# Group sums from TensorE to VectorE, one expert's product added by a DMA, and image 0's epilogue in halves

## The reference, cut to what matters

```python
def _gn(v, G=32, eps=1e-05):            # mean and variance over 4 channels and the plane
    g = v.reshape(B_, G, C_ // G, H_, W_)
    ...
# block 1, on n = gn(x): a convolution mixed from four experts by image
routing = sigmoid(mean(n, (2, 3)) @ w_route.T + b_route)          # (16, 4)
y = conv3x3(n, w_experts)                                         # 4 experts, 128 -> 128
out = einsum('beohw,be->bohw', y, routing)
h = x + silu(batchnorm(out))
# block 2, on n = gn(h): a convolution with the signs of W
result = h + conv3x3(gn(h), sign(W))
```

## Time and profile before

| what | value |
|---|---|
| median of three runs | 272.57 us |
| the profiled execution, its own time | 272.72 us |
| its span | 270.6 us |
| PE busy | 263.6 us, 97% |
| DVE busy | 254.6 us, 94% |
| ACT busy | 213.0 us, 79% |
| POOL busy | 45.5 us, 17% |
| granted TensorE clock | full in all 40 slices (2.4 GHz) |
| DMA queue of POOL (q0), share of the 16 DMA engines | 33.1% |

### The profile page before, as it was taken

The page is one execution under the profiler, slowest core; times in us unless marked ns, Lnnn a source line. Parts: engine busy times, 40 slices in busy tenths (PEclk is TensorE's granted clock), DMA queues, the critical chain, the costliest instruction groups (busy, mean ns, idle before and its releaser), DMA issues.

```text
span 270.6 us, 4214 instructions
## 1 busy us (share of the span) xinstructions
PE 263.6 (97%) x1339; PEld 182.5 (67%) x1339; DVE 254.6 (94%) x461; ACT 213.0 (79%) x469; POOL 45.5 (17%) x61
## 2 busy tenths in 40 slices
PE   8899999999999999999999999999999999999993
PEld 7554857668595766759486776849576675948573
DVE  5799999999999999999999999999999999995984
ACT  2798898898979787997979798897979796736860
POOL 2012120313121120312112021212112021210120
PEclk9999999999999999999999999999999999999999
DMA  6998945552617355452726456261735536272407
GB/s 202 417 388 279 325 150 156 78 155 32 127 78 131 104 79 155 58 134 54 145 80 97 136 79 159 27 128 80 125 108 80 157 47 128 70 136 87 78 2 155
DMA packets 10245, 35.20 MB, mean 130 GB/s; under 512 B 1264, under 2 KB 1904, under 8 KB 10224
## 3 DMA queue, kind: packets, MB, share of 16 engines
q0 software_dynamic: 4176, 15.21, 33.1%
q1 hardware_dynamic: 5616, 19.34, 19.1%
q10 hardware_dynamic: 432, 0.39, 0.4%
HBM read 11.34 MB, written 16.25 MB: 102 GB/s over the span
## 4 chain that ended last, share of the span: by engine, by line
PE 95%; DVE 2%; issue 1%; POOL 0%; ACT 0%; DVEq 0%; POOLq 0%
PE pc L599 43%; PE pa L562 14%; PE pb L562 14%; PE pe_ L562 14%; PE pd L552 6%; PE pd L488 2%; PE ps L531 1%; PE ps L535 1%; DVE U L1178 0%; PE pa L636 0%; PE pb L636 0%; DVE X L1404 0%; PE pc L521 0%; POOL rstd L446 0%; DVE sums L1386 0%
## 5 line engine op out<-in xcount | busy, mean ns | idle before, releaser
L1188 DVE SCALAR_TENSOR_TENSOR U<-we,route,U 128x1152 f32<-128x1152 f32 x45 | 63.7, 1415 | 0.5
L599 PE MATMUL pc<-lo,ws 128*128 128x496 f16 (+3 forms) x270 | 62.0, 375 | 0.0
L599 PE MATMUL pc<-hi,ws 128*128 128x496 f16 (+3 forms) x270 | 59.8, 375 | 0.1
L599 PEld LDWEIGHTS pc<-hi,ws 128*128 128x128 f16 x270 | 26.4, 98 | 29.6 <-issue 0.5
L599 PEld LDWEIGHTS pc<-lo,ws 128*128 128x128 f16 x270 | 27.7, 106 | 26.3
L446 POOL TENSOR_TENSOR rstd<-ve,nhalf 128x2 f32<-128x2 f32 (+1 forms) x19 | 17.5, 923 | 141.4 <-ACT ve L856 120.1
L562 PE MATMUL pa<-V,UM 128*128 128x256 f32 (+1 forms) x180 | 40.7, 375 | 0.0
L562 PE MATMUL pb<-V,UM 128*128 128x256 f32 (+1 forms) x180 | 40.6, 375 | 0.0
L562 PE MATMUL pe_<-V,U 128*128 128x256 f32 (+1 forms) x180 | 40.5, 375 | 0.0
L562 PEld LDWEIGHTS pb<-V,UM 128*128 128x128 f32 x180 | 34.1, 190 | 5.5 <-issue 0.7
L562 PEld LDWEIGHTS pe_<-V,U 128*128 128x128 f32 x180 | 34.2, 190 | 3.9
(11 more groups left out here) (168 smaller groups left out, 400.9 us busy)
## 6 DMA issues: line engine op xcount, KB each, us to landing
X<-x SPq DMA_DIRECT2D x15, 512.0 KB, 5.6
out<-X SPq DMA_DIRECT2D x15, 512.0 KB, 2.6
out<-ev POOLq DMA_DIRECT2D x15, 512.0 KB, 5.5
X<-y POOLq DMA_DIRECT2D x14, 512.0 KB, 4.5
we<-w_experts SPq DMA_DIRECT2D x2, 768.0 KB, 8.2
ws_raw<-w_sign SPq DMA_DIRECT2D x1, 576.0 KB, 10.4
we<-w_experts SPq DMA_DIRECT2D x1, 512.0 KB, 6.2
out<-X SPq DMA_DIRECT2D x1, 384.0 KB, 3.0
```

The source lines that it names most:

```text
L599: mm = mm_(rows[:, r0 - first // W:r1 - first // W, c0:c1], ws[:, tap * C:(tap + 1) * C], plane((hi, lo)[part], i)[:, r0 + ky - 1:r1 + ky ...
L1188: v.scalar_tensor_tensor(out=nine(U[i % RING]), in0=expert(e), scalar=route[:, i, e:e + 1], in1=nine(U[i % RING]), op0=ALU.mult, op1=ALU.a ...
```

## The change

Five things are changed.

1. **Group sums on DVE.** For the chains 4 to 17 `group_stats` on PE goes. DVE does `group_sums(c)` instead: a shuffle of the four columns with partition p^1, an add, a shuffle with p^2, an add, each waiting for the one before by a semaphore. It stands behind `inner_rows(t+1)` (in slot 15 ahead of `sign_points`). `variances`, `deviation` and `centring` read the sums from SBUF with a factor 1/4; `bias` reads a copy `gmid` that a new ACT instruction makes (`middle_mean`).
2. **Expert 1 by ACT and a DMA.** For the images 3 to 15 DVE's `mix(i, 1)` goes. ACT writes route[1]*expert 1 to a tile `scaled` (`scale_second`, last in its slot) and POOL issues a DMA that adds it to U (`add_scaled`, last in POOL's slot).
3. **hi sooner.** ACT does `bias` and `split_hi` ahead of `deviation`, `centring` and `pads`.
4. **Image 0 in halves.** SiLU and residual of image 0 are done in two halves of the plane; the residual stands ahead of `all_rows(2)` in DVE's order.
5. **Signs in two parts**, four taps ahead of `variance(2)` and five between the SiLU halves.

`route_logits` also waits for the previous chain's `th`.

```diff
+SCALED_FROM = 3
+        def first_mix(i):
+            return 2 if i >= SCALED_FROM else 1
+        def by_shuffles(c):
+            return LAG < c < CHAINS - 1
+        def group_means(c, a, b):
+            return (gsum[:, c, a:b], 1.0 / GSIZE) if by_shuffles(c) else (gstats(c, a, b), 1.0)
...
# POOL
+            def add_scaled(i):
+                pool.wait_ge(mix_first, firsts_before(i) + 1)
+                pool.wait_ge(scaled_ready, i - SCALED_FROM + 1)
+                g.dma_start(flat(U[i % RING][:]), scaled[:], accum_op=ALU.add).then_inc(scaled_added, 16)
...
                 if ND <= t < B and t not in DVE_RESIDUAL:
                     residual(t)
+                if t + LAG - 1 < B:
+                    add_scaled(t + LAG - 1)
...
# PE, slot t
                 if t < B:
                     minus_points(t)
                     if t > 1:
-                        group_stats(c)
                         sign_half(t - 2, 1, 1, TAP_ORDER[-1:])
...
# ACT
+            def wait_group(c):
+                if by_shuffles(c):
+                    act.wait_ge(gsum_ready, c - LAG)
+                else:
+                    act.wait_ge(gvar_ready, c + 1)
...
+            def middle_mean(c):
+                activation(gmid[:, c:c + 1], gsum[:, c, MID:MID + 1], ACT.Copy, scale=1.0 / GSIZE) \
+                    .then_inc(gmid_ready, 1)
...
+            def scale_second(i):
+                wait(act, scaled_added, 16 * (i - SCALED_FROM))
+                activation(scaled[:].rearrange("p (g n) -> p g n", n=C), expert(1), ACT.Copy,
+                           scale=route[:, i, 1:2]).then_inc(scaled_ready, 1)
...
+            def first_silu(half):
+                act.wait_ge(bn_ready, 5)
+                act.wait_ge(direct_ready, half + 1)
+                activation(flat3(y[0][:])[:, half * BANK:(half + 1) * BANK], direct_bank(0)[:, half, :], ACT.Silu,
+                           bias=bn_shift[:, 0:1], scale=bn_direct[:, 0:1],
+                           accum_out=(ysum[:, 0:1], first_ysum[:])[half]).then_inc(silu_ready, 1)
...
             centring(2)
+            sign_weights(0, 4)
             variance(2)
...
             mix(2)
-            sign_weights()
-            silu(0)
-            mean_mid(0)
+            first_silu(0)
+            first_half_mean()
+            sign_weights(4, K * K)
+            first_silu(1)
+            first_mean()
...
                 variances(c)
+                if t > 1:
+                    middle_mean(c)
                 if t > 1:
                     copy_minus(t)
                     evacuate(t - 2)
+                bias(c, MID)
+                split_hi(t - 1)
                 deviation(c)
                 if c < B:
                     centring(c)
                     pads(c)
-                bias(c, MID)
-                split_hi(t - 1)
-                if c < B:
                     pooled_plane(c)
                 split_hn(t - 1)
...
                 if c < B:
                     routing(c)
                     mix(c)
+                    scale_second(c)
...
# DVE
+            def group_sums(c):
+                a, step = 0, 1 if c < B else 3
+                data = stats[:, c, 0:4:step]
+                if c < B:
+                    dve.wait_ge(nm_in_ready, c + 1)
+                dve.wait_ge(nm_mid_ready, c - LAG + 1)
+                dve.wait_ge(spread_ready, columns_to(c))
+                for n, bit in enumerate((1, 2)):
+                    source = (data, pairs[:, 0:4:step])[n]
+                    target = (pairs[:, 0:4:step], gsum[:, c, 0:4:step])[n]
+                    wait(dve, pairs_ready, c - LAG - 1 + n)
+                    v.stream_shuffle(swapped[:, n, 0:4:step], source, [p ^ bit for p in range(32)]) \
+                     .then_inc(swapped_ready, 1)
+                    dve.wait_ge(swapped_ready, 2 * (c - LAG - 1) + n + 1)
+                    op = v.tensor_tensor(target, source, swapped[:, n, 0:4:step], ALU.add)
+                    op.then_inc((pairs_ready, gsum_ready)[n], 1)
...
             for t in range(1, B):
 
                 if t == B - 1:
+                    group_sums(t + LAG - 1)
                     sign_points()
+                if t == 1:
+                    first_residual()
                 all_rows(t + 1)
-                if t == 1:
-                    residual(0)
                 inner_rows(t + 1)
+                if 1 < t < B - 1:
+                    group_sums(t + LAG - 1)
                 transform_minus(t + 1)
```

More of the change, by code:

```diff
@@ L157, in build @@
         centre = sb("centre", [C, B, 2])
+        scaled = sb("scaled", [C, K * KCO])
         pooled = sb("pooled", [C, B, E])
+        swapped = sb("swapped", [C, 2, 4])
+        pairs = sb("pairs", [C, 4])
+        gsum = sb("gsum", [C, CHAINS, 4])
+        gmid = sb("gmid", [C, CHAINS])
         th = sb("th", [C, B, E])
@@ L282, in mixes_before @@
         def mixes_before(t):
-            return len(DIRECT_PARTS) * (E - 1) * min(t, ND) + (E - 1) * rank(t)
+            return len(DIRECT_PARTS) * (E - 1) * min(t, ND) + sum(E - first_mix(i) for i in range(ND, t))
+        def first_mix(i):
+            return 2 if i >= SCALED_FROM else 1
         def firsts_before(t):
@@ L353, in h_before @@
         def h_before(i):
-            return sum(1 for j in DVE_RESIDUAL if j < i)
+            return sum(2 if j == 0 else 1 for j in DVE_RESIDUAL if j < i)
         def wait_h(eng, i):
-            if i == B - 1:
+            if i in (0, B - 1):
                 eng.wait_ge(h_ready, h_before(i) + 2)
@@ L366, in silus @@
         def silus(i):
-            return i + 1 + (i == B - 1)
+            return i + 2 + (i == B - 1)
         def his(i):
@@ L529, in group_stats @@
                 wait_bank(c)
[L530 to L531 removed]
+                mm_(gstats(c, 0, 4), gmat[:], stats[:, c, 0:4], start=True, stop=True).then_inc(gvar_ready, 1)
             def route_logits(i):
                 pe.wait_ge(pooled_ready, i + 1)
+                if i > LAG:
+                    pe.wait_ge(th_ready, i)
                 mm_(logits(i), ones[:], pooled[:, i, :], start=True, stop=True).then_inc(logits_ready, 1)
@@ L829, in deviation @@
                     act.wait_ge(nm_in_ready, c + 1)
-                    activation(dev[:, c:c + 1], gnm(c, IN), ACT.Identity, bias=nm(c, IN), scale=-1.0) \
+                    mean, share = group_means(c, IN, IN + 1)
+                    activation(dev[:, c:c + 1], mean, ACT.Identity, bias=nm(c, IN), scale=-share) \
                         .then_inc(dev_ready, 1)
@@ L841, in variance @@
                 last = c == CHAINS - 1
-                act.wait_ge(gvar_ready, c + 1)
+                act.wait_ge(gvar_ready, LAG + 2 if last else c + 1)
                 activation(ve[:, c, k:k + 1], gvar(c, k), ACT.Identity, bias=epsilon[:, last:last + 1],
                            scale=1.0 / (HW * (LAST_SCALE if last else ACT_SCALE) ** 2)).then_inc(ve_ready, 1)
+            def wait_group(c):
[3 more added lines that the diff above has]
+                    act.wait_ge(gvar_ready, c + 1)
             def variances(c):
                 a, b = cols(c)
-                act.wait_ge(gvar_ready, c + 1)
-                activation(gdev2[:, c, a:b], gstats(c, a, b), ACT.Square, bias=base[:, 0:1]).then_inc(gdev2_ready, 1)
+                wait_group(c)
+                means, share = group_means(c, a, b)
+                activation(gdev2[:, c, a:b], means, ACT.Square, bias=base[:, 0:1],
+                           scale=share).then_inc(gdev2_ready, 1)
                 act.wait_ge(gdev2_ready, c - LAG + 1)
@@ L855, in variances @@
                 for k in range(a, b):
-                    op = activation(ve[:, c, k:k + 1], gvar(c, k), ACT.Identity, bias=less[:, c, k:k + 1],
-                                    scale=1.0 / (HW * ACT_SCALE ** 2))
+                    spreads, share = group_means(c, 3 - k, 4 - k)
+                    op = activation(ve[:, c, k:k + 1], spreads, ACT.Identity,
+                                    bias=less[:, c, k:k + 1], scale=share / (HW * ACT_SCALE ** 2))
                 op.then_inc(ve_ready, 1)
+            def middle_mean(c):
+                activation(gmid[:, c:c + 1], gsum[:, c, MID:MID + 1], ACT.Copy, scale=1.0 / GSIZE) \
+                    .then_inc(gmid_ready, 1)
             def bias(c, k):
                 act.wait_ge(rstd_ready, c + 1)
-                activation(nbias[:, c, k:k + 1], gnm(c, k), ACT.Copy,
+                if by_shuffles(c):
+                    act.wait_ge(gmid_ready, c - LAG)
+                activation(nbias[:, c, k:k + 1], gmid[:, c:c + 1] if by_shuffles(c) else gnm(c, k), ACT.Copy,
                            scale=rstd[:, c, k:k + 1]).then_inc((nbias_mid_ready, nbias_in_ready)[k], 1)
@@ L917, in mix_first_part, with sign_weights @@
                            scale=route[:, i, 0:1]).then_inc(mix_first, 1)
-            def sign_weights():
+            def sign_weights(first, last):
                 act.wait_ge(ws_loaded, 16)
```

(12 more changed lines are left out.)

45 lines of the change are left out of this document (34 added, 11 removed).

## The result

The changed kernel takes 279.69 us (median of 4 runs, 279.35 to 280.64) where the kernel before takes 272.66 (4 runs): a ratio of 1.0253, 95% interval 1.0232 to 1.0275. It is 7.0 us slower. Slower was forecast, by the mechanism that the traces then showed, but at 275.9 us and with a range up to 278.7: the forecast loss is half of the measured one.

A forecast was written before the change was run, and what follows sets the result against it. PE bounds the kernel at 15.50 us a slot; after the change ACT with its hand-off would, at 15.77. Entry +0.3, slots +3.0, tail -0.24, SBUF reads +0.3 give +3.4 us: 275.9 us, range 272.0 to 278.7.

The forecast's parts named there:

- PE sets the end, ACT is second by its idle time and not by its busy share: Kernel before, slots 2 to 15: PE without a gap for 15.50 us; ACT's own work 13.54 us a slot.
- ACT's new slot, 13.54 + 1.16 + 0.14 + 0.93 = 15.77 us, and 0.03 for reads from SBUF: ACT's loop: own work, scaled product, middle_mean and hand-off to DVE exceed PE's 15.38 us; SBUF reads add 0.03 a slot.
- 3.0 us for 11 slots: Slots 2 to 13: each of 11 cycles costs +0.27 us against the 15.50 us of the kernel before.
- Entry, +0.3 us: Start to slot 2: image 0 in halves removes slot 1's waiting, but hi of slot 2 comes 0.3 us later.
- Expert 1's DMA costs nothing: POOL and DMA: 576 KB in about 5.1 us, its reader some 9 us later; issue covered, otherwise 0.3 us.
- DVE in time by 0.2 us: DVE stands at the shuffles 14.6 us after gdev, ACT's spread comes at 14.84 us.
- hi sooner gives a phase and no period: ACT's order in the closed chain: earlier hi gives PE 0.69 us once, not in every slot.
- Tail, -0.24 us: From slot 13 on ACT falls under PE again; the two last group statistics save 2 x 0.12 us.
- The range: Whole kernel: 272.0 to 278.7 us, leaving out most of the short hand-off rival and the far part of the late-DVE-or-DMA one.
- the hand-off's upper bound: Spread to gdev: 1.2 us if a shuffle takes twice a small instruction; the whole would then be 278.9 us.
- The rule of the Trainium skill that was weighed: DVE's four hand-off instructions: an estimated 65 ns each, 0.26 us together, ACT staying under PE; the sum used trace rows instead.
- The rival that rested on short instructions: Between h's spread and gdev: hand-off short, PE stays the bound, 2.2 us saved, 270.4 us; chance 0.16.

The follow-up runs named there:

- e6_mix2_late: The changed kernel with DVE's addition of expert 1 of image 2 moved behind the inverse transform in slot 1: 278.63 us, ratio 1.0220.
- e7_old_order: The changed kernel with bias and split_hi behind deviation, centring and pads again (part 3 undone): 279.43 us, ratio 1.0248.
- e8_filled: The changed kernel with expert 1 of image 2 late, copy_minus and evacuate ahead of variances, and deviation, centring and pads ahead of bias: 271.25 us, ratio 0.9945.
- e9_minus_first: The changed kernel with only copy_minus moved ahead of variances on ACT, into its wait for DVE's sums: 273.80 us, ratio 1.0039.
- e10_filled_alone: The changed kernel with copy_minus and evacuate ahead of variances, deviation, centring and pads ahead of bias, expert 1 of image 2 unmoved: 271.95 us, ratio 0.9975.
- e5_longer_handoff: The changed kernel with each of the two additions of DVE's group sums done twice: 284.23 us, ratio 1.0422.
- e4_five_taps: The changed kernel with ACT and the DMA doing five of expert 1's nine taps and DVE the other four: 274.68 us, ratio 1.0061.

## Why the prediction was wrong in size

By its own steps:

- *PE sets the end, ACT is second by its idle time and not by its busy share*: right. In the changed kernel PE waits for hi in slot 1 (0.92 us) and in the slots 3 to 13 (0.19 to 0.55), and ACT's idle ahead of SiLU is gone.
- *ACT's new slot, 13.54 + 1.16 + 0.14 + 0.93 = 15.77 us, and 0.03 for reads from SBUF*: the step that failed. Measured it is 13.71 + 1.15 + 0.10 + 1.02 = 15.98. 0.09 us are the hand-off: the four instructions start 0.20, 0.20, 0.19 and 0.20 us apart, as the pair of the earlier trace rows had it, and the mask loads are nearly hidden, but 0.23 us pass from the end of the spread to the first shuffle (0.21 to its mask load), where I had left 0.03 for both ways between engines. 0.17 us, not 0.03, are the small ACT instructions that read gsum: the two of ve hold ACT for 0.38 us where they held it for 0.30, gdev, deviation and nbias for 0.03 or 0.04 more each. middle_mean and the scaled product came 0.05 cheaper. An error of 0.18 us in a slot of 16 against the 15.80 of the sum, times 11: 2.0 us.
- *3.0 us for 11 slots*: 5.8, of which those 2.0, and 0.5 from three slots that were longer for once. In the longest, DVE's shuffle starts 0.36 us after its mask load with no wait shown; it recurs in the same slot in e6_mix2_late, e7_old_order, e8_filled, e9_minus_first and e10_filled_alone, not in e5_longer_handoff, where another slot is the longest. In the closed loop it adds 0.34 us to the slot, in e8_filled, where PE is the bound, 0.20. What it comes from wasn't tried. In the second a small ACT instruction (stats) waits 0.18 us for the one before it, in the third the power takes 1.32 us instead of 0.72.
- *Entry, +0.3 us*: +1.1. The removed wait did go, but the front moved POOL's power to the start of a 1.41 us instruction of DVE: 1.94 us instead of 1.12, shown by e6_mix2_late. The 0.82 us are what the entry was short of.
- *Expert 1's DMA costs nothing*: right, 4.8 us to landing, no wait for it on DVE, and no fixed cost in e4_five_taps. *DVE in time by 0.2 us*: right, by 0.31 (its wait for the spread).
- *hi sooner gives a phase and no period*: right, e7_old_order.
- *Tail, -0.24 us*: -0.14 by the trace, and in part by luck: hi of slot 13 to hi of slot 14 takes 15.62 us and not the 15.38 that were foretold, the next slot 15.23 for 15.25.
- The range: it rests on the hand-off's upper bound alone, 1.2 us, which by the prediction's own sum is 278.9 and above the range's top of 278.7. Nothing was left for the small instructions, a slot that is late for once, or the entry, and these are 0.14 us a slot, 0.5 us and 0.8 us.

The rule of the Trainium skill that was weighed ("VectorE: DVE Perf Modes", "The TRN2 errata", 58 cycles and the elements) falls here: a shuffle of 4 elements takes 0.16 us and not 0.065, and linked ones follow at 0.20. The same section says that this row gives too little and that the fixed term measures near 150 cycles; with that the estimate for 4 elements is 0.16 us, and the trace agrees. The rival that rested on short instructions went with it, and e5_longer_handoff gives their real price.

## What to carry to other kernels

Before work is moved off the bound, close the loop: add up the occupied time of the second engine in one period, waits between dependent small instructions and hand-offs included, and compare that with the bound's period; the two here, ACT's 15.98 us and PE's 15.38, were within 4%, and against a forecast loss of 0.27 us a slot an error of 0.18 is two thirds. A wait on an engine is free only while another engine sets the period; once it doesn't, fill the wait with work that is due anyway (0.48 us filled took 0.48 us off), which here, with one DVE instruction of slot 1 moved, turned the same change from 2.5% slower into 0.5% faster (0.25% without that move). Small instructions, in number and in what memory they read, belong in the sum with their start-to-start distance.

## What the runs showed of the hardware

**A small GpSimd instruction waits for VectorE's.** The power of two columns took between 0.70 and 1.94 us in the slots 1 to 13 of the two kernels and the experiments, mostly 0.72 or 0.80. In the changed kernel's slot 1 DVE's addition of expert 1 stands beside it:
```profile
33.43 0.69 DVE L1354 TENSOR_TENSOR V<-e_rows 128x512 f32<-128x512 f32 x1
34.03 1.41 DVE L1285 SCALAR_TENSOR_TENSOR U<-we,route,U 128x1152 f32<-128x1152 f32 x1
```
The power ends at 36.01, 0.57 us after that instruction's end at 35.44, and alone, near the start of the kernel, it takes 0.55. In e6_mix2_late the instructions beside it are shorter or read PSUM, and it takes 0.70. It is no single case: in each of the slots 1 to 13 of both kernels, 26 in all, the power ends 0.56 to 0.58 us after the end of a DVE instruction with two inputs in SBUF. The third of the late slots is one of them (211.82 to 212.39, 0.57 us):
```profile
211.14 0.68 DVE L1354 TENSOR_TENSOR V<-e_rows 128x512 f32<-128x512 f32 x1
```
```profile
211.07 1.32 POOL L473 TENSOR_TENSOR rstd<-ve,nhalf 128x2 f32<-128x2 f32 x1 [2.35 <-ACT ve L899]
```
The Trainium skill ("SBUF — State Buffer", "Who interferes with whom") has a rule that fits: a VectorE instruction with two inputs in SBUF shuts out a GpSimd instruction that reads SBUF until it is done. By it the power of slot 1 waits 1.37 us and then takes its 0.55, 1.92 us in all, and 1.94 were measured: the trace agrees.

**Price of sums over four partitions on VectorE.** Two shuffles and two additions on four columns in the changed kernel:
```profile
176.95 0.16 DVE L1252 STREAM_SHUFFLE swapped<-stats 128x4 f32<-128x4 f32 x1
177.15 0.16 DVE L1255 TENSOR_TENSOR pairs<-stats,swapped 128x4 f32<-128x4 f32 x1
177.35 0.01 DVE L1252 LOAD_MASK_SELECT swapped<-pairs  x1
177.35 0.15 DVE L1252 STREAM_SHUFFLE swapped<-pairs 128x4 f32<-128x4 f32 x1
177.54 0.17 DVE L1255 TENSOR_TENSOR gsum<-pairs,swapped 128x4 f32<-128x4 f32 x1
```
0.76 us from the first shuffle to the sums, 1.02 us as seen by the engine that asks; PE's matmul, when PE was ready for it, took 0.60 us as seen by the same engine.
